# Two-layer block with adaptive layer norm: routed rows without the gate row, accumulators joined on chip at the end, and every engine's instruction order laid out anew

## The reference, cut to what matters

```
x: 8 samples x 256 tokens x 256 features, f32
layer 0: h = layernorm(x)*(1+ca)+sa; x += ga * attention(h)      16 heads of 128, 4 key/value heads, causal
         h = layernorm(x)*(1+cb)+sb; x += gb * (routed(h) + shared(h))   8 experts, top 2, hidden 176
layer 1: h = layernorm(x)*(1+ca)+sa; x += ga * linear_attention(h)
         h = layernorm(x)*(1+cb)+sb
         t = rms_norm(h)*norm_w
         G = softmax over the top 4 of (t @ gate_w.T + gate_b), 16 experts, 0 elsewhere
         a, b = even and odd columns of t @ w1[e].T + b1[e], clipped at 7
         act  = a * sigmoid(1.702 a) * (b + 1)
         x += gb * (h + sum_e G[:, e] * (act @ w2[e].T + b2[e]))
```

## Time and profile before

| | |
|---|---|
| median of 3 runs | 1031.97 us (1031.87 to 1034.49) |
| the profiled execution | 1035.23 us, of which the span from first to last instruction is 1033.1 us |
| PE, PEld busy | 966.9 us (94%), 818.0 us (79%) |
| DVE, ACT, POOL busy | 725.7, 673.3, 426.7 us |
| moved by DMA | 180.53 MB, mean 175 GB/s |

### The profile page before, as it was taken

One profiled execution on the slowest core, in us unless ns is written; L12 is line 12 of the kernel. 1 busy time (PEld: TensorE's weight loads), 2 busy tenths in 40 slices (PEclk: granted clock), 3 DMA queues, 4 the chain that ended last, 5 costly groups with the idle time before them and its releaser, 6 DMA issues.

```text
span 1033.1 us, 20537 instructions
## 1 busy us (share of the span) xinstructions
PE 966.9 (94%) x6036; PEld 818.0 (79%) x6036; DVE 725.7 (70%) x2546; ACT 673.3 (65%) x1944; POOL 426.7 (41%) x447
## 2 busy tenths in 40 slices
PE   8999999999999999999999999996879889999980
PEld 5769878878988887887888788885767679999970
DVE  3564656787767687777669677865888678888870
ACT  2757767668677767768767875783746457777740
POOL 3322411421461362255146136323166646565662
PEclk9999999999999999999999999998999899999995
DMA  9927991993799420020012004237258788999954
GB/s 307 305 87 243 376 375 69 355 378 131 287 363 378 174 79 1 22 94 22 1 67 70 2 12 165 64 131 281 61 164 184 208 238 219 222 223 223 217 111 81
DMA packets 93677, 180.53 MB, mean 175 GB/s; under 512 B 9901, under 2 KB 29037, under 8 KB 92669
## 3 DMA queue, kind: packets, MB, share of 16 engines
q1 hardware_dynamic: 73467, 148.55, 43.2%
q0 software_dynamic: 18752, 30.30, 13.1%
q10 hardware_dynamic: 1346, 0.36, 0.2%
HBM read 77.71 MB, written 107.99 MB: 180 GB/s over the span
## 4 chain that ended last, share of the span: by engine, by line
PE 81%; DVE 7%; issue 4%; DMA 3%; ACT 1%; POOL 1%; another core or an unknown queue 1%; ACTq 1%; SPq 0%; DVEq 0%; POOLq 0%
PE bank L1112 12%; PE bank L1076 10%; PE bank L1048 10%; PE bank L1121 5%; PE bank L1066 5%; PE bank L1038 5%; PE bank L1027 4%; PE bank L998 3%; PE bank L1067 3%; PE bank L1057 2%; PE bank L1037 2%; PE bank L913 2%; PE bank L904 2%; PE bank L982 2%; PE bank L1020 2%
## 5 line engine op out<-in xcount | busy, mean ns | idle before, releaser
L1908 POOL TENSOR_TENSOR RB<-RB 128x512 f32<-128x512 f32 x64 | 66.7, 1042 | 277.1 <-DVE RB L1687 276.7
L1112 PE MATMUL bank<-RB 128*128 128x128 f32 x1264 | 157.3, 278 | 5.3 <-DVE BC L1801 2.3
L1112 PEld LDWEIGHTS bank<-RB 128*128 128x128 f32 x1264 | 150.4, 194 | 8.3 <-DVE BC L1801 3.4
L1377 ACT ACTIVATE RB<-RA,nw 128x512 f32 x158 | 105.4, 715 | 48.9 <-issue 22.3
L1076 PE MATMUL bank<-RA,RB 128*128 128x256 f32 x512 | 132.5, 381 | 1.1 <-ACT RB L1278 1.1
L1048 PE MATMUL bank<-RA 128*128 128x256 f32 x512 | 121.4, 380 | 0.3 <-DMA RA<-in_L_attn_Wq 0.3
L1048 PEld LDWEIGHTS bank<-RA 128*128 128x128 f32 x512 | 94.6, 190 | 15.6 <-issue 2.8
L1076 PEld LDWEIGHTS bank<-RA,RB 128*128 128x128 f32 x512 | 91.3, 190 | 14.4 <-issue 2.3
L1884 POOL TENSOR_TENSOR qs<-qs,half 128x4 f32<-128x4 f32 x64 | 65.6, 1024 | 63.8 <-DVE qs L1696 56.1
L1121 PE MATMUL bank<-RB,BC 128*128 128x256 f32 x316 | 83.1, 387 | 8.3 <-DVE BC L1814 7.3
L1278 ACT ACTIVATE RB<-bank 128x256 f32<-128x256 f32 x128 | 48.7, 381 | 45.8 <-PE bank L1067 43.9
(11 more groups left out here) (254 smaller groups left out, 2416.3 us busy)
## 6 DMA issues: line engine op xcount, KB each, us to landing
xsD<-BC SPq DMA_DIRECT2D x17, 4232.0 KB, 32.8
RB<-in_w2b SPq DMA_DIRECT2D x79, 256.0 KB
RB<-xsD SPq DMA_DIRECT2D x61, 264.5 KB
BC<-modD SPq DMA_DIRECT2D x16, 512.0 KB, 4.1
X<-xsD SPq DMA_DIRECT2D x18, 264.5 KB, 3.2
RA<-in_w SPq DMA_DIRECT2D x2, 2048.0 KB, 7.2
RA<-in_w SPq DMA_DIRECT2D x6, 512.0 KB, 8.6
RA<-in_L_attn_Wq SPq DMA_DIRECT2D x1, 2048.0 KB, 13.9
```

The source lines that it names most:

```text
L1112: m = pe.matmul(ps[:, 128 * j:128 * j + 128], WS[:, n % 2, c, 128 * j:128 * j + 128], XT[:, n % 2, c * 128:c * 128 + 128], start=(c == 0), ...
L1377: m = act.activation(WS[:, n % 2, c, :], W1[:, bass.ds(r, 1), c, :].rearrange("p a n -> p (a n)"), ACT.Copy, scale=nw[:, c:c + 1])
L1908: pool.tensor_tensor(sq, qrow, qrow, ALU.mult).then_inc(mine("q_sq", p), 1)
```

## The change

- `ROW` goes from 529 to 273: the gate row is no longer in the table. `f_gb` and its waits go. `y_out` multiplies by the gate and 0.5 alone.
- `y_add` adds into two DRAM accumulators, `accA` and `accB`, both cleared at the start (`acc_zero` is two stores of 2 MB). `store` goes, with the waits on it in `xb` and `y_add`. The tokens stay in `X`.
- The row buffers of the first 22 blocks move out of `X`; the loads of blocks 2 to 4 now wait for `s_x(6, 1)`, that of block 1 for the last `q_t`, instead of that of block 4 for the latter.
- `gains` (SP) loads `gb` of all samples, broadcast to 128 partitions (1 MB), during block 38.
- `merge` goes. After the last two `y_add` have landed, SP loads `accA` and ACT `accB` in 8 pieces of 256 KB each. Per sample a `join` adds the two, multiplies by the gain and adds the tokens: three operations on 128x512, on DVE for six samples and on POOL for samples 2 and 5. SP stores each result (`put`, 256 KB).
- The planner's allowances, weights and landing times are other numbers, and its allowances have separate values before and after the last attention unit. So every engine's order before the loop of 57 blocks is another; the loop's own order is the same, but for `gains`.

```diff
-NBLK, REG, ROW = 79, 2048 + 128, 529
+NBLK, REG, ROW = 79, 2048 + 128, 273
+JOIN_POOL = 2, 5
-DURING, BEHIND = {5: 0, 6: 0}, {5: -1.1, 6: 0, 7: 0}
+ALLOWED = {"keys": (0.048, -1.364), "query": (0.001, -1.211), "first": (0.1, -0.191), "shared": (0.045, 0.04), "dense": (0, 0.036), "linear": (0.089, -0.035), "late": (0.621, -0.907), "route": (0.1, -0.146), "gain": (0.027, -0.821), "count": (0.148, 0.019), "weights": (-0.523, -1.847), "token": (0.687, 0.979), "unit": (0.1, 1.452), "block": (0.212, 0.157), "turn": (0.603, -0.02)}
+DURING, BEHIND = {5: 0, 6: -0.27, 7: 0.01}, {5: 6.55, 6: 0.36, 7: -0.09}
...
-    KV, QUERY, FIRSTS, SHARED, DENSE, LINEAR, LATE, UNIT, FILL, TURN = 0.04, 0, 0.1, 0.04, 0.0, 0.08, 0.1, 0.1, 0.2, 0.18
...
-        after = [("n_bi", 0), ("store", PART - 1), ("f_send", 1, PART - 1, 1, 3)] + [("q_t", NU // 2 - 1)] * (n == RINGS[0] - 1) + ...
+        after = [("n_bi", 0), ("f_send", 1, PART - 1, 1, 3)] + [("q_t", NU // 2 - 1)] * (n == 1) + [("s_x", NB - 2, 1)] * (1 < n < RINGS[0]) + ...
...
-    p.add("merge", by=16)
+        if n == lo + 16:
+            p.add("gains", by=16)
+    for b in range(NB):
+        p.add("sum_a", b, slot=b, by=16)
+        p.add("sum_b", b, slot=b, by=16)
+    for b in range(NB):
+        p.add("join", b, slot=b in JOIN_POOL)
+        p.add("put", b, by=16)
...
-        YB = [free[:, 1280 + 256 * i:1536 + 256 * i] for i in range(3)] + [RB[:, 5120:5376], X[:, 0:2 * PART, :].rearrange("p t n -> p (t n)")[:, 2304:2560]]
-        XB = ([X[:, 0:2 * PART, :].rearrange("p t n -> p (t n)")[:, 530 * i:530 * i + 530] for i in range(4)] + [RC[:, 4944:5474]],
-              [RC[:, 530 * i:530 * i + 530] for i in range(RINGS[1])])
+        YB = [free[:, 1280 + 256 * i:1536 + 256 * i] for i in range(3)] + [RB[:, 5120:5376], RC[:, 5218:5474]]
+        XB = ([SC[:, 9880:9880 + ROW], RC[:, 4944:4944 + ROW]] + [BC[:, 0, 274 * i:274 * i + ROW] for i in range(3)],
+              [RC[:, 274 * i:274 * i + ROW] for i in range(RINGS[1])])
...
+            def sum_a(b):
+                on.wait_ge(*done("w_in", NBLK - 1))
+                on.wait_ge(*done("y_add", NBLK - 1 - NBLK % 2))
+                on.wait_ge(*done("y_add", NBLK - 2 + NBLK % 2))
+                sp.dma_start(sumA[:, 2 * b:2 * b + 2, :], acc_v[0][:, 2 * b:2 * b + 2, :]).then_inc(mine("sum_a", b), 16)
+            def put(b):
+                on.wait_ge(*done("join", b))
+                sp.dma_start(out_v[:, b, :, :], sumA[:, 2 * b:2 * b + 2, :]).then_inc(mine("put", b), 16)
...
-                act.activation(route(1)["src"][:, :, 273:529], row(1, b, 768), ACT.Copy, scale=0.5).then_inc(mine("f_gb", b), 1)
...
-                dve.scalar_tensor_tensor(YB[n % 5], psum("y_out", n)[:, 0:256], rows(n)[:, bass.ds(ex[n] + 257, 1)], rows(n)[:, 273:529], ALU.mult, ALU.mult).then_inc(mine("y_out", n), 1)
+                dve.tensor_scalar(YB[n % 5], psum("y_out", n)[:, 0:256], rows(n)[:, bass.ds(ex[n] + 257, 1)], 0.5, ALU.mult, ALU.mult).then_inc(mine("y_out", n), 1)
...
+            def join(b):
+                if (b in JOIN_POOL) != False:
+                    return
+                t, x = sumA[:, 2 * b:2 * b + 2, :], X[:, 2 * b:2 * b + 2, :]
+                on.wait_ge(*done("sum_a", b))
+                on.wait_ge(*done("sum_b", b))
+                dve.tensor_tensor(t, t, sumB[:, 2 * b:2 * b + 2, :], ALU.add).then_inc(ch.sem, ch.up())
+                on.wait_ge(*done("gains"))
+                on.wait_ge(ch.sem, ch.n)
+                dve.tensor_tensor(t, t, gains[:, b:b + 1, :].broadcast_to([128, 2, 256]), ALU.mult).then_inc(ch.sem, ch.up())
+                on.wait_ge(ch.sem, ch.n)
+                on.wait_ge(*done("f_x", b))
+                dve.tensor_tensor(t, t, x, ALU.add).then_inc(mine("join", b), 1)
...
-                pool.indirect_dma_start((out_r, accD)[n % 2], bass.IndirectOffsetOnAxis(to[:, n % 6:n % 6 + 1], 0), YB[n % 5], None,
+                pool.indirect_dma_start((accA, accB)[n % 2], bass.IndirectOffsetOnAxis(to[:, n % 6:n % 6 + 1], 0), YB[n % 5], None,
```

More of the change, by code:

```diff
@@ L119, in allowance @@
     def allowance(self, c):
-        late, of = c[2].get("late", c[0]), c[4]
-        return late + (BEHIND if ("wo", NU - 1) in self.end else DURING).get(of, 0.0)
+        kind, of, behind = c[2].get("late", c[0]), c[4], ("wo", NU - 1) in self.end
+        return ALLOWED[kind][behind] + (BEHIND if behind else DURING).get(of, 0.0)
     def begin(self, c):
@@ L268, in mod_rows @@
                 yield do("bc", 1, b, slot=4 + b, by=16, aside=True)
-            p.chain(LATE, no_rows())
+            p.chain("late", no_rows())
         else:
@@ L289, in unit @@
         if u + 1 < NU:
-            p.chain(UNIT, unit(u + 1))
+            p.chain("unit", unit(u + 1))
         yield do("s_max", u, bank=1 + u % 2, last=True, after=[("q_rs", u // 2)] + [("p_t", u - 4)] * (u >= 4))
@@ L300, in unit @@
         if h == 0 and b + 1 < NB:
-            p.chain(KV, att_kv(b + 1))
+            p.chain("keys", att_kv(b + 1))
         if h == 15:
             yield do("res", 0, b, bank=5, last=True, after=[("bc", 0, b)])
-            p.chain(FIRSTS, ffn0(b), b)
+            p.chain("first", ffn0(b), b)
     def ffn0(b):
@@ L315, in ffn0 @@
         for i in range(2):
-            p.chain(SHARED, shared(b, i), b)
+            p.chain("shared", shared(b, i), b)
         yield do("f_top", 0, b, after=[("f_sig", b, 0), ("f_sig", b, 1)])
@@ L413, in offsets @@
         if b + 2 < NB:
[L414 removed]
+            yield do("bc", 1, b + 2, slot=4 + b % 2, by=16, aside=True)
         yield do("f_x", b)
[L416 removed]
     def spread(part):
@@ L468, in rest_begins @@
             yield do("xb", n, slot=RINGS[0] + (n - FIRST) % RINGS[1], by=16, aside=True, after=[("f_send", 1, NB - 1, 1, 3), ("n_bi", 1), ("wo1", NB - 1)])
-            p.chain(LATE, rest_turned(n))
+            p.chain("late", rest_turned(n))
     def rest_turned(n):
@@ L478, in load_block @@
         p.add("xb", n, slot=RINGS[0] + (n - FIRST) % RINGS[1], by=16)
-    p.chain(KV, start_h())
-    p.chain(KV, start())
-    p.chain(LATE, fill())
-    p.chain(FIRSTS, mod_rows(0))
-    p.chain(QUERY, queries())
-    p.chain(UNIT, unit(0))
-    p.chain(LATE, last_weights())
+    p.chain("keys", start_h())
+    p.chain("keys", start())
+    p.chain("late", fill())
+    p.chain("first", mod_rows(0))
+    p.chain("query", queries())
+    p.chain("unit", unit(0))
+    p.chain("weights", last_weights())
     for steps in (weights_in(), weights_out(), block(0)):
-        p.chain(FILL, steps)
-    p.chain(LATE, rest_begins())
+        p.chain("block", steps)
+    p.chain("weights", rest_begins())
     p.run()
@@ L541, in build @@
         macc_set = ctx.enter_context(nc.semaphore("macc_set"))
-        own = {e: ctx.enter_context(nc.semaphore(f"{e}_own")) for e in ("dve", "act")}
+        own = {e: ctx.enter_context(nc.semaphore(f"{e}_own")) for e in ("dve", "act", "pool")}
         def done(stage, *key):
@@ L865, in _ @@
                     run[stage](*key)
-            on.wait_ge(*done("store", NB - 1))
-            on.wait_ge(*done("merge"))
+            on.wait_ge(*done("put", NB - 1))
         @block.tensor
```

110 lines of the change are left out of this document (57 added, 53 removed), and 10 rows, old and new, of the table ENGINE.

## The result

The changed kernel takes 1038.93 us (median of 14 runs, 1035.52 to 1040.29), the kernel before beside it 1033.21 us (14 runs, 1031.60 to 1038.07): a ratio of **1.0047, 95% interval [1.0034, 1.0061]**. It is slower by half a per cent; 1026.3 us was predicted, with 0.22 on slower, and a range that ended at 1038. The profiled execution of the changed kernel took 1038.55 us, with a span of 1036.5.

What follows compares the result with a forecast made beforehand. PE was taken as the bound, except 28.3 us idle from 700 to 850 and 30.0 us behind the last matmul. -4.7 + 7 - 8 = -5.7 us took the median from 1031.97 to 1026.3 us, range 1011 to 1038.

Steps and rivals of the forecast that it cites:

- loop of 57 blocks: 850 to 995 us: shorter rows lower the DMA share to about 0.75, but PE is full, so 0 gain.
- drain of the additions: Behind the last matmul: POOL's additions no longer lag, so the last lands at 1009.8 instead of 1014.5, -4.7 us.
- end behind the last landing: From the last addition's landing to the span's end: loads, joins and stores replace the merge, +7 us (+1.9 to +7.9).
- 700 to 850: First 22 blocks beside the last samples' other stages: shorter rows and new order, -8 us (-18 to +10).
- if time goes with bytes: In 700 to 850: row-transfer and scatter-time chain pieces, 17.75 us together, lose 8.9 us as row bytes halve.
- The data alone: At the end: 6.29 MB of loads and stores, without joins' time, end 20.4 us behind the last addition's landing.
- rival A: At the end: joins exclude each other, stores wait, the gain is eaten; 1039.9 us, or 1035.2 with the -4.7; chance 0.17.
- D: Before 700: the new order is worse, one idle us in a hundred costs +6.5, giving 1038 us; chance 0.05.
- Rival C: Whole kernel a wash: end gives -4.7 and takes 5, the rest 0; 1031 to 1033 us; chance 0.15.

Runs made afterwards that it cites:

- two-operation kernel: Kernel before's order with short rows, two accumulators, X/gb + h stored into accumulator A beforehand, each join one addition and one product on DVE: 1023.94 us, ratio 0.9997.

## Why the prediction was wrong, step by step

| step | forecast us | measured us | |
|---|---|---|---|
| loop of 57 blocks | 0 | 0 | PE 145.00 of 145 in both |
| drain of the additions | -4.7 | -4.0 | 7.4 for 11.4 behind the last matmul |
| end behind the last landing | +7 | +6.6 | |
| 700 to 850 | **-8** | **+0.8** | the last matmul comes later; the step that failed |
| sum, on the profiled span | -5.7 | +3.4 | |

The +0.8 is small by the choice of executions: the profiled one of the kernel before took 1035.23 us, 2.0 above its median of 1033.21, the changed kernel's 0.4 below its own. Between the medians lie 5.7 us; with -4.0 and +6.6 for the drain and the end, +3.1 is left for 700 to 850. On the last chip it is 7.8 us of medians, less -3.6 and +7.1: +4.3, where the traces have +1.7. (An estimate, as if drain and end were alike in all executions.) The forecast for this stretch was off by 9 to 12 us.

**The step that failed is "From 700 to 850".** It let 17.75 us of the chain, transfers and unknown waits, go about by half as the bytes of a row do, and gave the new order, for want of rows, a place in the bounds but nothing in the sum. *The rows.* In the old order the short rows alone are worth 5.4 us, of which the drain is 3.0 to 3.4 (8.0 us behind the last matmul; 11.0 in the kernel before on the last chip, 11.4 on the first) and the end 0.3 (18.0 for 18.3); some 2 us, about what the interval leaves open, remain for all that comes before. On one chip the two-operation kernel, in the old order, with its own store per sample, issues its last scatter at 816.9 and the kernel before at 815.6. At most those 2 of the 8.9 us of "if time goes with bytes" are there. The pieces of the earlier trace rows did leave the chain: among the 195 longest pieces from 690 to 850 the changed kernel has no transfer and no unknown wait, nor has the kernel before with short rows in the same order. Taking a wait off the chain did not give its length back. Nor do these transfers go with the bytes: a block's row load took 3.2 us at the median for 264.5 KB and 3.1 us for 136.5 KB, over all blocks, and on the last chip 3.7 and 3.1 us in the loop. The loop of the changed kernel:

```profile
q1 hardware_dynamic: 14885, 20.63, 50.4%
...
RB<-xsD SPq DMA_DIRECT2D x46, 136.5 KB, 3.0
SC<-modD SPq DMA_DIRECT2D x1, 1024.0 KB, 8.4
```

*The order.* PE's idle time from 700 to 850 fell by 6.1 us, but its busy time for the same 6036 instructions rose by 7.1, and 7.1 - 6.1 is about the 0.8 us by which the last matmul came later. On the other chip: 6.6 us less idle, +7.0 of busy time, last matmul +1.7. I had reckoned PE's idle time as what can be won and its busy time as fixed. The busy time depends on the granted clock, and in the new order there is more low clock, and it meets dearer products. That the clock is the whole of the 7 us can be worked out from the traces: take, for each stretch of 1 us, PE's busy time times what the granted clock lacks of 1, and add them up. It is 6.9 us in the kernel before and 13.9 in the changed one, +7.0 of +7.1; on the last chip 2.1 and 9.2, +7.1 of +7.0. Some 4 us of either lie between 700 and 740, the rest between 740 and 850. The mean granted clock of the whole span says the same for every run: 0.9722 for the changed kernel with its joins on DVE (12 runs) beside 0.9783 for the kernel before, 0.9767 with nothing joined (9 runs) beside 0.9822; these two have an end about as long as the kernel before's, and 0.006 of the span is 6 us. In the old order the changed kernel with its joins on DVE has 0.9820 beside 0.9822. No kernel held the order and changed the clock alone, and why the clock falls a second time isn't shown.

Part of the 7 us comes and goes from execution to execution. The trace with nothing joined has a busy sum of 966.6 us with the same 0.78 from 720 to 740 and full clock behind 740; it is of the fastest of that kernel's nine runs, with a mean clock of 0.980 where the others have 0.974 to 0.978.

**The end** was right to 0.4 us (to 0.1 on the last chip), and by the reason given: DVE and POOL exclude each other (the earlier trace rows had one meeting of 2.31 us; now operations of 0.69 us take 1.63 to 1.75 us, and POOL's of 1.08 1.26 to 1.59), and taking POOL's share away gives 2.1 us. The data alone, forecast at 20.4, took 21.2. The mistake was only of weight: at +7 this was the largest term with a row behind it, and I set it against a larger term that had none.

The Trainium skill (SBUF — State Buffer, section Who interferes with whom) calls the pair of ports that DVE and GpSimd share an exclusive lock, and says that a DVE instruction with two SBUF inputs contends with a GpSimd one that reads SBUF. The trace agrees: DVE's operation of 1022.46 ended at 1024.09, 0.55 us behind POOL's of 1021.95, about as if it had begun only then, and its 0.69 us became 1.63.

**The drain** came to -4.0 of -4.7, by the mechanism given: POOL isn't behind at the end, since the additions of one accumulator can follow each other faster than two blocks of PE. The short rows do it, not the second accumulator: with `out` and `accD` as before it is 8.0 us, in the old order with two accumulators 7.9. The new order has 7.4 in its four traces; why it has 0.5 less I don't know. Here is the loop of the changed kernel, to stand beside the earlier trace rows:

```profile
979.96 1.56 POOL L1987 DMA_INDIRECT accA<-BC,to  x1 [0.32 <-POOL to L1978]
...
982.92 1.56 POOL L1987 DMA_INDIRECT accB<-BC,to  x1 [1.20 <-DVE RB L1821]
...
984.85 1.56 POOL L1987 DMA_INDIRECT accA<-RB,to  x1 [0.18 <-POOL to L1978]
```

These two additions into `accA` follow at 4.89 us, where the earlier trace rows had 5.89 with a wait of 1.86 for a landing. (It is no lasting pace: on average an accumulator gets one per two blocks of PE, 5.74 us.) On the last chip the additions' medians from issue to landing in the loop fell from 4.8 to 5.0 us to 4.5 to 4.8. Three details missed: the DMA share of the loop is 0.82, not 0.75 (the rows and weights' queue fell from 60.7% to 50.4%, by 10 points where the rows' bytes promised 15; the 1 MB of `gains` is in it); POOL still sits idle for about 1 us before every other addition, now because it is early; and `y_out` takes 0.48 us as before, not 0.43, which cost nothing.

**The rivals.** It ended as rival A, "the end eats the gain", in its version with the -4.7: 1035.2 was its time for a transition that gives nothing, and the ratio, 1.0047 of the 1031.97 us that the forecast stood on, is 1036.8. (The measured 1038.93 stands beside 1033.21 for the kernel before in the same comparison.) A had 0.17. (The 0.22 on slower is the whole of A and D, though the text puts a part of A within no change.) The price of A was right and its chance too low: the only thing against it was a transition gain that no row priced. Rival C had 0 for the transition as well, but an end of +5 less 4.7.

## What to carry to other kernels

A stretch's idle time on the bounding engine is a ceiling, not an income: ask what its busy time will do, for where the granted clock is low in and behind the gaps, the same work takes more time, and it matters which products stand there. A forecast sum should take each term at the weight of its rows; if the sign hangs on a term that no row prices, take that term at zero and let the priced ones decide. And before an order that a planner made is compared, hold it: a stage of 0.6 us per sample taken off its list moved the end by 8 us or more, and hid a gain of 5.

## What the runs showed of the hardware

- DVE and POOL on 128x512 f32 with two inputs in SBUF: 0.69 us alone on DVE, 1.63 to 1.75 beside POOL. Two samples of eight handed to POOL cost 2.1 us instead of giving some.
- Loads of 256 KB that are issued 16 at once land after 8.0 and 8.6 us at the median, in the kernel with two-operation joins; in the changed one DVE can start on the first pair 3.6 us behind its issue (1011.41 to 1014.97). The joins can't start together; they follow the queue.
- POOL's closing drain behind a merge of 2 MB, DRAM to DRAM, is 17.83, 17.48 and 17.15 us in three traces, and each ends 4.1 us behind the start of SP's, which waited for the merge to land. With two-operation joins and no merge POOL's drain takes 7.43 us from 1000.2, long before the end.
- One kernel on three chips had medians of 1035.04, 1025.20 and 1023.62 us. Of the stretches behind 700 the one from 820 to 850 differs most: PE 23.05 of 30 us at a clock of 0.94 in the kernel before on the chip of the first profile, 26.18 at 1.00 on the last. Times differ by 1.1%; the changed kernel's ratio in its two comparisons was 1.0047 and 1.0062, with intervals that meet.
